# Denominators spread by a matrix multiply into PSUM, and projections spread evenly over the pairs of an attention loop

## What is computed

```python
def rational_softmax(scores, eps=EPS):
    num = 0.5 * (1.0 + scores * jax.lax.rsqrt(1.0 + scores * scores))
    return num / (jnp.sum(num, axis=-1, keepdims=True) + eps)
...
scores = jnp.einsum('bhtd,bhsd->bhts', q, k) * scale     # D = 32
scores = scores + alibi
scores = jnp.where(causal[None, None], NEG, scores)
probs = rational_softmax(scores, EPS)
out = jnp.einsum('bhts,bhsd->bhtd', probs, v)
```

## Time and profile before

| | us |
|---|---|
| median of 3 runs (2229.65 to 2236.6) | 2234.24 |
| the profiled execution, its own time | 2231.39 |
| its span | 2229.5 |
| engine busy: PE, DVE, ACT, POOL | 1768.5, 1805.8, 1713.3, 1691.9 |
| groups 0 to 7, from their first L1135 to the next group's | 248.1, 225.1, 225.3, 240.4, 330.5, 224.3, 225.3, 251.8 |
| from the last pair to the end | 126.9 |
| mean granted PE clock | 0.922 |

### The profile page before, as it was taken

One profiled execution on the slowest core, in us unless ns is written; L12 is line 12 of the kernel. 1 busy time (PEld: TensorE's weight loads), 2 busy tenths in 40 slices (PEclk: granted clock), 3 DMA queues, 4 the chain that ended last, 5 costly groups with the idle time before them and its releaser, 6 DMA issues.

```text
span 2229.5 us, 29232 instructions
## 1 busy us (share of the span) xinstructions
PE 1768.5 (79%) x10640; PEld 897.9 (40%) x10640; DVE 1805.8 (81%) x1730; ACT 1713.3 (77%) x1842; POOL 1691.9 (76%) x720
## 2 busy tenths in 40 slices
PE   5668877777787789999987888886887687897765
PEld 4554433333333336565443443332333233443331
DVE  4238888988889889889785878888889888998838
ACT  0037998889888988878775878898889888897652
POOL 2027888888888887778775877888888888897738
PEclk9899989988988899999998998998999899999889
DMA  5411101110111022211323121210112012222146
GB/s 179 148 49 45 49 21 45 40 49 20 45 41 49 21 68 74 68 34 40 97 63 92 43 77 40 50 54 16 35 47 58 15 46 76 52 61 60 46 165 207
DMA packets 126602, 138.49 MB, mean 62 GB/s; under 512 B 27868, under 2 KB 78044, under 8 KB 126044
## 3 DMA queue, kind: packets, MB, share of 16 engines
q1 hardware_dynamic: 126460, 136.64, 21.6%
HBM read 54.02 MB, written 22.80 MB: 34 GB/s over the span
## 4 chain that ended last, share of the span: by engine, by line
PE 38%; DVE 21%; ACT 21%; issue 11%; POOL 4%; SPq 3%; DMA 2%; DVEq 0%; POOLq 0%; ACTq 0%
ACT yb L748 8%; DVE gb L1135 7%; DVE gb L1066 7%; PE sc L917 7%; ACT gb L713 6%; PE it L817 6%; PE ov L896 6%; ACT yb L750 5%; PE dn L896 5%; PE it L834 4%; PE it L841 3%; PE it L821 3%; SPq L473 3%; POOL oT L707 2%; DMA area<-in_x_dram 1%
## 5 line engine op out<-in xcount | busy, mean ns | idle before, releaser
L674 POOL TENSOR_TENSOR yb<-yb 128x1024 f32<-128x1024 f32 x544 | 1503.0, 2776 | 432.6 <-DVE gb L1135 415.0
L748 ACT ACTIVATE yb<-sc 128x1024 f32<-128x1024 f32 x544 | 551.6, 1014 | 310.8 <-PE sc L917 185.6
L1135 DVE TENSOR_TENSOR gb<-sc,yb 128x1024 f32<-128x1024 f32 x544 | 662.4, 1218 | 142.8 <-ACT yb L750 139.1
L1066 DVE TENSOR_TENSOR gb<-gb,yb 128x1024 f32<-128x1024 f32 x544 | 773.9, 1423 | 0.1
L917 PE MATMUL sc<-qmv,kst 128*128 128x512 f32 (+3 forms) x1280 | 482.8, 461 | 263.0 <-DVE gb L1135 250.5
L750 ACT ACTIVATE yb<-yb 128x1024 f32<-128x1024 f32 x544 | 575.5, 1058 | 17.2
L713 ACT ACTIVATE gb<-gb 128x1024 f32<-128x1024 f32 x544 | 566.2, 1041 | 0.0
L917 PEld LDWEIGHTS sc<-qmv,kst 128*128 128x128 f32 x1280 | 231.5, 202 | 568.1 <-DVE gb L1135 412.0
L896 PE MATMUL ov<-gb,vv 128*32 128x512 f32 (+3 forms) x2560 | 326.4, 594 | 29.5 <-DVE den L1080 24.6
L896 PE MATMUL dn<-gb,ones 128*32 128x512 f32 (+3 forms) x2560 | 312.5, 572 | 0.0
L817 PE MATMUL it<-hT,wT 128*128 128x512 f32 x496 | 245.2, 627 | 8.2 <-ACT area L728 3.2
(11 more groups left out here) (113 smaller groups left out, 1086.9 us busy)
## 6 DMA issues: line engine op xcount, KB each, us to landing
qmv<-stage SPq DMA_DIRECT2D x384, 64.0 KB
kst<-stage SPq DMA_DIRECT2D x384, 64.0 KB
area<-in_x_dram SPq DMA_DIRECT2D x58, 256.0 KB, 2.8
out_dram<-oT SPq DMA_DIRECT2D x32, 256.0 KB, 3.2
den<-rec_d SPq DMA_DIRECT2D x31, 256.0 KB
wT<-wT_d SPq DMA_DIRECT2D x7, 768.0 KB, 4.4
x_d<-area SPq DMA_DIRECT2D x16, 256.0 KB, 2.6
z_d<-area SPq DMA_DIRECT2D x16, 256.0 KB, 2.7
```

What stands on the lines that cost most here:

```text
L674: pool.tensor_tensor(y, y, y, ALU.mult).then_inc(s_y2, 1)
L748: act.activation(yview(n), sc[:, n % SLOTS], ACT.Square).then_inc(s_s2, 1)
L1066: dve.tensor_tensor(gview(n), gview(n), yview(n), ALU.add).then_inc(s_num, 1)
L1135: dve.tensor_tensor(gview(n), sc[:, n % SLOTS], yview(n), ALU.mult).then_inc(s_g, 1)
```

## The change

1. The budget for each pair goes from 1.61 + slack to 0.9 + slack. For the plain groups (slack 0) fewer parts fit a pair; in the others slack is raised by 0.7, so that the sum stays as it was (within 0.01).
2. The start and due pairs of the projections are written out. In the list of a plain group a burst of two items at pair 61 and a whole item at pair 11 are gone, parts mostly come one or two to a pair, and q of chunk 1 is made at the end of the group before (pairs 64 to 67) instead of at pair 0.
3. The way back of the inverses: SP copies `rec` by one transfer into `rrow`, 4 partitions x 512 (L548 of the new file), not over DRAM. PE multiplies it with a constant 4x128 matrix `heads` (ones where the row belongs to the head) into an item bank (new item "n", one part, 6 pairs after the copy of `ov` or a little later), and DVE multiplies `oT` by that bank (L1117). Regroup, inversion and transfer stand 1, 2 and 3 pairs after the copy.
4. PE waits for `rrow` (s_row), SP's transfer into `rrow` for the division before (s_norm), SP's regroup for the last `rrow` transfer; items o are planned after the item n of their chunk. In group 7 they may start 3 pairs earlier.

```diff
+        f, end = self.first, len(self.pairs) - 1
+        over = [f[3] + 2 * TT * (c + 1) for c in range(2)]
+        wanted = [(("q", 1), 0, 0), (("k", 1), 0, 8), (("v", 1), 0, 13)] if opens else []
+        wanted += [(("q", 2), f[1] + 1, f[2] - 5), (("k", 2), f[1] + 2, f[2] + 8), (("v", 2), f[1] + 3, f[2] + 10),
+                   (("q", 3), f[2] + 1, f[3] - 5), (("k", 3), f[2] + 2, f[3] - 3), (("v", 3), f[2] + 3, f[3])]
+        if has_next:
+            wanted += [(("q", 0, "next"), f[3] + 1, f[3] + 16), (("k", 0, "next"), over[0] + 1, end - 8),
+                       (("v", 0, "next"), over[0] + LAG, end - 6), (("k", 1, "next"), over[1] + 1, end - 4),
+                       (("v", 1, "next"), over[1] + LAG, end - 2), (("q", 1, "next"), end - 4, end)]
...
+        norms += [Job(("n", c), [0.86], (), self.last[c] + LAG + NORM, self.last[c] + LAG + NORM + 1) for c in range(n_chunks - 1)]
...
-            left = max(-1.0, min(left, 0.5)) + 6 * CH / 1200 - 0.95 + slack
+            left = max(-1.0, min(left, 0.5)) + 0.9 + slack
...
-            def regroup_back(G, c):
+            def rows(G, c):
 
                 n = G * NC + c
                 sp.wait_ge(s_rec, n + 1)
-                sp.dma_start(rec_d.rearrange("h (a n) -> (h a) n", n=HG * CH // P), rec[:, :]).then_inc(s_den, 16)
-                sp.wait_ge(s_den, 48 * n + 32)
-                sp.dma_start(den[:, :], rec_d.unsqueeze(1).to_broadcast([HG, D, CH])).then_inc(s_den, 16)
+                if n:
+                    sp.wait_ge(s_norm, n)
+                sp.dma_start(rrow[:, :].rearrange("h (a n) -> h a n", n=HG * CH // P), rec[:, :]).then_inc(s_row, 16)
...
+                if what == "n":
+                    pe.wait_ge(s_row, 16 * ((G - (len(job.name) == 3)) * NC + c + 1))
+                    return pe.matmul(bank, heads[:, :], rrow[:, :], start=True, stop=True)
...
-            def divide(G, hg, c):
-                dve.wait_ge(s_den, 48 * (G * NC + c) + 48)
-                dve.wait_ge(s_out, G * NC + c + 1)
+            def divide(i, bank, G, hg, c):
+                dve.wait_ge(s_item, i + 1)
                 o = out_slice(hg, c)
-                dve.tensor_tensor(o, o, den[:, :], ALU.mult).then_inc(s_norm, 1)
+                dve.tensor_tensor(o, o, bank, ALU.mult).then_inc(s_norm, 1)
```

More of the change, by code:

```diff
@@ L138, in __init__ @@
                 made.setdefault((job.name[1] // TT, 0 in chunks), []).append(job)
[L141 to L156, removed]
@@ new lines, in __init__ @@
+        if has_next:
+            wanted += [(("q", 0, "next"), f[3] + 1, f[3] + 16), (("k", 0, "next"), over[0] + 1, end - 8),
+                       (("v", 0, "next"), over[0] + LAG, end - 6), (("k", 1, "next"), over[1] + 1, end - 4),
+                       (("v", 1, "next"), over[1] + LAG, end - 2), (("q", 1, "next"), end - 4, end)]
+        projections, staged = [], None
+        for name, start, until in wanted:
+            after = made.get((name[1], len(name) == 3), []) + ([staged] if name[0] != "v" and staged else [])
+            projections.append(Job(name, [0.86] * 4, after, start, until, EVAC if name[0] == "v" or not staged else STAGED))
+            if name[0] != "v":
+                staged = projections[-1]
@@ new lines, in __init__ @@
+        norms = [] if opens else [Job(("n", n_chunks - 1, "prev"), [0.86], (), LAG - 1 + NORM, LAG + NORM)]
+        norms += [Job(("n", c), [0.86], (), self.last[c] + LAG + NORM, self.last[c] + LAG + NORM + 1) for c in range(n_chunks - 1)]
+        for job in others:
+            if job.name[0] == "o":
+                job.after += tuple(n for n in norms if n.name[1] == job.name[1] // TT and (len(n.name) == 3 or not has_next))
+        tracks = [[job for job in others if job.name[1] % 2 == 0], [job for job in others if job.name[1] % 2], projections, norms]
@@ L229, in joined @@
                           min(over - 1 if i < 2 else over + 8, first[NC] - 1))
-    joining = Group(NC, [job for j in range(KB) for job in joined(j)], True, slack=0.8)
+    joining = Group(NC, [job for j in range(KB) for job in joined(j)], True, slack=1.5)
     assert all(job.at <= first[job.name[1] // TT + 1] + LAG - 2 for job in joining.items if job.name[0] == "o")
@@ L809, in compute @@
                     if job.needs:
-                        emptied(job.needs - 1, of, dve_base, act_base)
+                        emptied(job.needs - 1, of, dve_base, act_base, norm_base)
                     elif what == "q" and len(job.name) == 2:
@@ L869, in project_first @@
                 for part in range(KC):
-                    r = compute(bank, Job((what, 0), []), part, 0, 0, None, 2 * TT, 0, wqT_s[:, 0])
+                    r = compute(bank, Job((what, 0), []), part, 0, 0, None, 2 * TT, 0, wT=wqT_s[:, 0])
                 r.then_inc(s_item, 1)
@@ L911, in group @@
                             if k == at:
-                                own = g.operands.index((what, c)) + 1 if (what, c) in g.operands else -(c == 0 and carry)
+                                own = g.operands.index((what, c)) + 1 if (what, c) in g.operands else -2 * (c == 0 and carry)
                                 pe.wait_ge(s_op, 16 * NPROJ * (ops_before(g, G) + own))
```

106 lines of the change are left out of this document (62 added, 44 removed).

## The result

The changed kernel takes 2193.1 us (median of 4 runs, 2189.0 to 2195.0), the kernel before in the same series 2234.5; the ratio is 0.982, interval 0.980 to 0.983. That is 41 us less, where 86 were forecast. The time lies in the forecast's range (2108 to 2205), but 45 us above its likeliest value of 2148, so the sum needs an explanation.

A forecast was written before the change was run, and what follows sets the result against it. No engine alone bounds the kernel; ACT sets a plain group's floor of 200.6 us, late pairs add 25. Savings 48 + 9 + 6 + 11 + 12 = 86 us gave 2145 for the profiled execution, so 2148; range 2108 to 2205.

The forecast's parts named there:

- The 14.6 of the terms: Plain group: sum of savings in us over its late pairs and the inversion of chunk 1, before deductions leaving 12.
- the 1.5 forecast: Plain groups, inversion of chunk 1: DVE would still wait about 1.5 us instead of 2.76, saving about 1.1.
- opening's 2.5 for k of chunk 1: Opening group: k of chunk 1 moves from the start, where everything waits for PE, to pair 3, saving 2.5 us.
- Pair 0: q of chunk 1 at 1.31 becomes q at pair 67 for 0.78 ... Saves 0.9: Plain group: moving q of chunk 1 to pair 67 also removes PE's burst with it, saving 0.9 us.
- the forecast 6: Closing group: PE bounds it, not more than 11 us can go, 6 us saving taken.
- Joining's 11: Joining group: 11 us saved in all, from pair 21, the divisions and the burst at 61, less q's parts.
- At pair 21 q no longer stands before the adapter's items, 5: Joining group, pair 21: q no longer ahead of the adapter's items saves 5 us.
- Item o of tile 3 now needs the bank of tile 2's: 1 to 2 at most: Joining group, longest pair, 9: the residual load keeps its place, so 1 to 2 us at most.
- The 7.37 at item o of tile 8: Ending group: PE's 7.37 us wait for the division after pair 53 mostly goes with n at pair 50, saving 6.
- The division still waits for POOL: Rival: the division stays at 2.38 us, only the bursts gain, about 55 us in all, 2179; chance 0.05.
- PE becomes the bound: Rival: parts of n land on the path where PE's clock is slow, 40 us come back, 2188; chance 0.2.
- The slower rival: At 31 items n, PE waits for a late `rrow` behind other SP work; up to 2288 us; chance 0.07.

The follow-up runs named there:

- e4: Changed kernel, but the division multiplies by `den` in SBUF instead of the bank in PSUM (outputs not the kernel's): 2225.1 us.
- e1: Changed kernel with the first loads of closing and joining issued before the 13 transfers of q of chunk 1: 2163.4 us, ratio 0.970.
- e2: Kernel before, with the first loads of closing and joining issued behind the 13 transfers of q of chunk 1: 2271.7 us, ratio 1.017.
- e9: e1 with two pairs of neighbours exchanged in joining, w2/3 ahead of zt/2 and n/0 ahead of zt/3: 2156.5 us, ratio 0.964.
- e5: e1 with joining's projections and other items in the old order, q of chunk 1 still at the end of closing: 2149.5 us, ratio 0.962.
- e10: e1 with a planner rule: no item begins in the pair where the item two places before was made, if ACT empties that one: 2130.6 us, ratio 0.954.
- e8: e5 with four transposes in each plain-group pair that has neither part nor product: 2151.6 us against 2149.5.
- e3: The new division alone, with the kernel before's starts, ends and budgets of projections and groups: 2250.5 us, ratio 1.010.

## Why the prediction was wrong

- **The division.** Right: 678 ns in the median, 31 times, and e4 shows that the operand's space is the cause.
- **The plain groups.** Right in kind and small: 15.4 us a group where 12 were forecast. The 14.6 of the terms came whole; the 2.6 taken off for parts of n and for what POOL wins back were not paid (POOL is busy for 191.6 us in group 2, as before, 191.5). The inversion of chunk 1 is 1.8 to 1.9 late in three of the four groups, near the 1.5 forecast, and 2.89 in group 2, where its heap hardly shrank (the "10.8 us after they began" behind that 1.5 is 10.7 by rows 6). That POOL lies 0.14 us a pair behind ACT was read from its 2.81 us, which contain a wait for L1066 (above).
- **Up to the first pair.** Priced inside opening's 2.5 for k of chunk 1; in fact 12.9. In the kernel before, DVE waited for q's transfers before it could empty k, ahead of its first L1135:

```profile
129.21 0.69 DVE L993 TENSOR_SCALAR stage<-it 128x512 fp32r<-128x512 f32 x1 [10.76 <-DMA qmv<-qal]
```

  All runs with the old plan have 129 to 131 us here, all with the new one 118 to 119. The trace of before held the row; I had looked for changed instructions there, not for a wait that moves. The remaining 6.5 of opening's 9 came as 5.4.
- **Closing and joining: the step that failed.** "Pair 0: q of chunk 1 at 1.31 becomes q at pair 67 for 0.78 ... Saves 0.9" priced DVE and PE and left out SP: the wait for transfers that q's move delays was put at nothing, without a reason. The item takes 13 transfers with it, and before two groups it passed the loads of the next group's first tiles, which SP had issued 13 us ahead of the group and now issues 6 us into it. TensorE waited 10.45 and 14.54 us for them. Closing lost 14 by it and joining 14 (e1), and e2 puts the same loss into the old kernel. With the loads in front, closing is 234.4: the forecast 6, within a spread of 6.
- **Joining's 11.** "At pair 21 q no longer stands before the adapter's items, 5" did not happen: 16.8 us there, 16.2 before. "Item o of tile 3 now needs the bank of tile 2's: 1 to 2 at most" looked at the right kind of wait at one pair only. At pairs 16 and 18 banks changed owner from DVE to ACT (e9). Of the 22 us that e1 still loses, the order costs some 12 (e5, just over the spread), and e10's order gives 36. Joining came out 47 us above its forecast (+36 for -11), the loads' 14 included: it is the largest error of the sum.
- **Ending.** The 7.37 at item o of tile 8 went as forecast (some 13 us back from pair 52 on), but +8 stood there by then. Some 3 of it came between pairs 20 and 28, which no run explains, and some 3 more at n of chunk 1, which waited 2.5 for `rrow`, and the clock fell.
- **The rivals.** "The division still waits for POOL" is out (e4), "PE becomes the bound" found no support (plain groups 208 to 211 at a clock of 0.93 to 0.94, e8). The slower rival is real, though not in this version: e3 has it in most groups, and one change of three pairs takes it away. I gave it 0.07; what kept it off was the order of 13 transfers and a 0.6 us one.

That the time lies inside the range is in part luck: the 12.9 us up to the first pair and 13.6 in the plain groups came beyond the forecast and made up for some 26 of the 73 us that the other parts fell short. The same holds for e1: with the two starts repaired the change gives 68 us, which is near 86 only with those 26.

## What to carry to other kernels

When an item is moved, write down for each in-order queue that it feeds what it now stands in front of, past the border of the stage too: the item's own cost was 0.78 us, what it stood in front of cost 28 in two groups. With few banks, what matters is who empties the bank of the item that many places before; a new small item shifts this for all behind it. An edit that gives nothing alone, or less than nothing, may gain once the other half is there: here the division alone made the kernel 1% slower, and with its transfer three pairs further from its use 0.4% faster.

## What was not expected of the hardware

- TensorE's clock: behind a wait of 3.22 us, and behind two of 2.21 and 2.01, products ran at 0.50 (1.94 in place of 1.06 us); in e3 the pair behind the wait for `rrow` cost POOL 2.71 us more, after 1.56 for the wait itself.
- The division with two SBUF inputs lasts 0.68 to 2.38 us in e4, by where POOL is in its instruction. In group 2 each of the four costs POOL 1.76, whether it lasted 1.00, 1.78 or 2.38.
- The same waiting is inside most pairs, in both directions: POOL's 128x1024 square takes 1.89 us by itself and 2.81 behind the start of L1066, and L1066 takes 1.22 by itself and up to 2.98 behind the start of POOL's.
- Filling TensorE's empty pairs with transposes raised its granted clock from 0.94 to 0.96 and the time by nothing.
